# Expert products taken two at a time with biases laid by matmuls, routing weights broadcast through DRAM, and the router's marks kept in PSUM

## What is computed

```python
logits = xt @ Wr + br                                  # 64 -> 8
probs = softmax(logits); top_p, top_idx = top_k(probs, 2)
weights = top_p / top_p.sum(axis=-1, keepdims=True)
xe = layernorm(xt)[None] * ln_g[:, None] + ln_b[:, None]
h = gelu(einsum('end,edh->enh', xe, W1) + b1[:, None])  # 64 -> 256, all 8 experts
y = einsum('enh,ehd->end', h, W2) + b2[:, None]         # 256 -> 64
out = (weights[:, :, None] * y_of_the_two_experts).sum(axis=1)
```

## Time and profile before

| | us |
|---|---|
| median of 3 runs | 408.23 (407.21 to 408.71) |
| the profiled execution, its own time | 409.93 |
| its span in the profile | 408.2 |
| VectorE busy | 337.5 (83%) |
| TensorE busy | 338.1 (83%) |
| ScalarE busy | 281.3 (69%) |
| GpSimd busy | 265.9 (65%) |
| all DMA queues, share of 16 engines | 62.7% |

### The profile page before, as it was taken

One profiled execution on the slowest core, in us unless ns is written; L12 is line 12 of the kernel. 1 busy time (PEld: TensorE's weight loads), 2 busy tenths in 40 slices (PEclk: granted clock), 3 DMA queues, 4 the chain that ended last, 5 costly groups with the idle time before them and its releaser, 6 DMA issues. The chain is left out here.

```text
span 408.2 us, 5461 instructions
## 1 busy us (share of the span) xinstructions
PE 338.1 (83%) x1642; PEld 181.1 (44%) x1642; DVE 337.5 (83%) x462; ACT 281.3 (69%) x458; POOL 265.9 (65%) x270
## 2 busy tenths in 40 slices
PE   0597897677999789888988997899789878998694
PEld 0484445333454445344534552455245424544352
DVE  2774458998999999999999999999999988995411
ACT  1002667498978987998799879987887757761462
POOL 9706112986569947994898589758975984593122
PEclk9996999589899999999999999999988986999899
DMA  8761079899899588658975697579667950000000
GB/s 195 204 134 26 2 189 223 216 227 224 203 222 227 138 206 205 163 123 197 219 177 137 153 239 169 146 174 220 151 162 176 230 124 0 2 0 13 2 0 13
DMA packets 21236, 59.52 MB, mean 146 GB/s; under 512 B 4924, under 2 KB 13272, under 8 KB 15320
## 3 DMA queue, kind: packets, MB, share of 16 engines
q1 hardware_dynamic: 20040, 58.34, 61.7%
q10 hardware_dynamic: 1168, 0.84, 0.8%
HBM read 53.93 MB, written 5.24 MB: 145 GB/s over the span
## 5 line engine op out<-in xcount | busy, mean ns | idle before, releaser
L345 POOL TENSOR_TENSOR hs<-hs,Cs 128x1024 f32<-128x1024 f32 x63 | 149.2, 2372 | 44.9 <-DVE hs L767 44.3
L767 DVE TENSOR_TENSOR_SCAN hs<-av,P 128x1024 f32<-128x1024 f32 x64 | 146.3, 2287 | 4.7 <-ACT av L576 1.3
L633 ACT ACTIVATE hb<-P,b1c 128x512 f32<-128x512 f32 x128 | 81.6, 684 | 18.8 <-PE P L1177 16.3
L760 DVE SCALAR_TENSOR_TENSOR P<-P,bbcol,ub 128x1024 f32<-128x1024 f32 x62 | 79.7, 1286 | 2.4 <-DMA ub<-u_scratch 1.2
L1190 PE MATMUL P<-hb,W2s 128*64 128x256 f32 x512 | 70.0, 397 | 0.0
L1176 PE MATMUL P<-X,W1H 128*128 128x512 f32 x128 | 60.4, 472 | 6.4 <-ACT hb L633 4.7
L576 ACT ACTIVATE av<-P,Aneg 128x510 f32<-128x510 f32 x68 | 44.1, 688 | 13.9 <-PE P L1130 10.0
L1177 PE MATMUL P<-X,W1L 128*128 128x512 f32 x128 | 52.3, 409 | 0.0
L357 POOL TENSOR_TENSOR accs<-accs,mes 128x256 f32<-128x256 f32 x56 | 40.9, 731 | 14.1 <-DVE mes L856 9.5
L1190 PEld LDWEIGHTS P<-hb,W2s 128*64 128x64 f32 x512 | 31.8, 138 | 31.4 <-issue 20.8
L856 DVE SCALAR_TENSOR_TENSOR mes<-P,cols,wbs 128x256 f32<-128x256 f32 x64 | 27.3, 468 | 17.4 <-PE P L1190 9.6
(11 more groups left out here) (190 smaller groups left out, 488.8 us busy)
## 6 DMA issues: line engine op xcount, KB each, us to landing
ub<-u_scratch SPq DMA_DIRECT2D x31, 1024.0 KB, 10.7
av<-dt_scratch SPq DMA_DIRECT2D x15, 1024.0 KB, 7.0
dt_scratch<-dts SPq DMA_DIRECT2D x7, 256.0 KB, 2.8
u_scratch<-rl SPq DMA_DIRECT2D x7, 256.0 KB, 2.8
av<-in_L_conv_Wr SPq DMA_DIRECT2D x2, 576.0 KB, 7.3
av<-in_L_conv_Wl SPq DMA_DIRECT2D x2, 576.0 KB, 8.1
res<-in_x SPq DMA_DIRECT2D x4, 256.0 KB, 4.8
hb<-in_L_ffn_W SPq DMA_DIRECT2D x2, 512.0 KB, 6.3
```

The lines of the kernel that those rows point to most:

```text
L345: gp.tensor_tensor(hs[:, at, :, :], hs[:, at, :, :], rep(Cs[:, p, :], 1, 2), ALU.mult).then_inc(S["cm"], 1)
L633: a_.activation(hb[:, r % 4, :], P[:, (XA, XB)[r % 2], :], ACT.Gelu, bias=b1c[:, r:r + 1]).then_inc(S["gl"], 1)
L760: v.scalar_tensor_tensor(out=ring, in0=rep(P[:, BB, :], 1, 2), scalar=bbcol[:, 0:1], in1=ub[:, 2 * n:2 * n + 2, :], op0=ALU.add, op1=ALU.m ...
L767: v.tensor_tensor_scan(hs[:, (SLOTS * g + n) % RING].rearrange("p a t -> p (a t)"), av[:, 2 * n:2 * n + 2, :].rearrange("p a t -> p (a t)" ...
```

## The change

Five things are done.

1. **Expert products.** One product with 512 columns takes the place of two with 256. The bias is no longer added there: TensorE opens each bank with a matmul of `b2w` by `b2sel` (64 rows, f32r, 512 columns), and the four matmuls of each of the four half steps add to it. `b2w` holds each bias in a high and a low part; both are built in the setup, from four more small DMAs and some 15 more VectorE instructions.
2. **Broadcast of the weights.** `selW`, the eight matmuls and the four ScalarE copies per body go. TensorE transposes the plain weights, ScalarE copies them to `wT` (16 x 256) and issues a DMA to `w_scratch` in DRAM. SP waits for its landing and issues six DMAs that fill `wbs` from it (1 MB in all), between piece 0 and piece 1 of the scan's loads. VectorE waits for the first two (`wb0`) at the first pair of experts, the next two (`wb1`) at the second, the last two (`wb2`) at the third.
3. **Router's marks.** The exponential and the ranked marks are written to PSUM (`chances`, `ranked`, in bank XC).
4. **Router's bias.** A matmul of `ident` by `brs` opens the bank, and the two logit matmuls add to it; L816 goes.
5. **Order.** The router's maximum and difference stand between the two halves of `X`; the layer norm product of group i+2 (`xnt<-P,rs`) stands inside the router. GpSimd's split of the weights (two instructions) goes.

```diff
@@ SP: sp_spread, and a new function
             for c in range(CHUNKS):
+                if c == 1 and g >= 2:
+                    sp_weights(sp_, g - 2)
                 since(sp_, "scan", SLOTS * (g - 1) + 2 * c + 2)
...
+        def sp_weights(sp_, g):
+
+            sp_.wait_ge(S["wt_out"], 16 * (g + 1))
...
+            since(sp_, "me", PAIRS * g)
+            for r, (lo, hi) in enumerate(((0, 2), (2, 4), (4, 8))):
+                for h in range(2):
+                    sp_.dma_start(wbs[64 * h:64 * h + 64, lo:hi, :],
+                                  rep(w_dram[g % 2][EXP * h + lo:EXP * h + hi, :], 0, 64)).then_inc(S[f"wb{r}"], 16)
@@ GpSimd: pool_router
+            since(eng, "wtr", 2 * g)
             gp.tensor_tensor(rt[:, 11], rt[:, 10], rep(rv[:, 5], 2, EXP), ALU.mult).then_inc(S["wn"], 1)
-            eng.wait_ge(S["wn"], g + 1)
-            w4 = rt[:, 11].rearrange("p (q h) e -> p q h e", h=2)
-            since(eng, "wtr", 2 * g)
-            gp.tensor_copy(vv[:, :, :, 0, :].bitcast(f32r), w4).then_inc(S["vhi"], 1)
-            eng.wait_ge(S["vhi"], g + 1)
-            gp.tensor_tensor(vv[:, :, :, 1, :], w4, vv[:, :, :, 0, :], ALU.subtract).then_inc(S["vlo"], 1)
@@ ScalarE
-            a_.activation(rt[:, 2], rt[:, 1], ACT.Exp).then_inc(S["ex"], 1)
+            a_.activation(chances, rt[:, 1], ACT.Exp).then_inc(S["ex"], 1)
...
-            a_.activation(wT[:, :], P[0:32, XD, 0:HW], ACT.Copy).then_inc(S["wtc"], 1)
-
-        def act_wb(eng, g, r):
-            eng.wait_ge(S["wb_mm"], EXP * g + 2 * r + 2)
-            if r == 0:
-                since(eng, "me", EXP * g)
-            a_.activation(wbs[:, 2 * r:2 * r + 2, :].rearrange("p e f -> p (e f)"), P[:, YS, :], ACT.Copy).then_inc(S["wb"], 1)
+            since(eng, "wt_out", 16 * g)
+            a_.activation(wT[:, :], P[0:2 * EXP, YS, 0:HW], ACT.Copy).then_inc(S["wtc"], 1)
+            eng.wait_ge(S["wtc"], g + 1)
+            since(eng, "wb2", 32 * (g - 1))
+            eng.dma_start(w_dram[g % 2], wT[:, :]).then_inc(S["wt_out"], 16)
@@ VectorE
+                if h == 1 and between is None:
+                    dve_router1(eng, g)
                 v.tensor_tensor(X2[0:64, HW * h:HW * h + HW], P[q, XB, 0:HW], rqs[q, :], ALU.mult).then_inc(S["xh2"], 1)
...
-            v.tensor_tensor(biased, P[:, XC, 0:4 * EXP].rearrange("p (c e) -> p c e", e=EXP),
-                            rep(brs[:, :], 1, 4), ALU.add).then_inc(S["lgb"], 1)
...
-            v.scalar_tensor_tensor(out=rt[:, 3], in0=rt[:, 2], scalar=1.0, in1=rank[:, :, :], op0=ALU.is_ge, op1=ALU.mult).then_inc(S["s1"], 1)
+            v.scalar_tensor_tensor(out=ranked, in0=chances, scalar=1.0, in1=rank[:, :, :], op0=ALU.is_ge, op1=ALU.mult).then_inc(S["s1"], 1)
...
             v.tensor_reduce(rv[:, 2], rt[:, 5], AX, ALU.max).then_inc(S["m2"], 1)
+            if norm is not None:
+                dve_xn(eng, norm)
...
-            v.scalar_tensor_tensor(out=mes[:, e % 4, :], in0=P[:, (XC, XD)[e // 2 % 2], HW * (e % 2):HW * (e % 2) + HW],
-                                   scalar=cols[:, R["b2"] + e:R["b2"] + e + 1], in1=wbs[:, e, :],
-                                   op0=ALU.add, op1=ALU.mult).then_inc(S["me"], 1)
+            j = e // 2
+            eng.wait_ge(S["f2"], EXP * KC * g + 2 * KC * (j + 1))
+            eng.wait_ge(S[f"wb{min(j, 2)}"], 32 * (g + 1))
+            since(eng, "acc", EXP * g + max(e - 2, 0))
+            v.tensor_tensor(mes[:, 2 * (j % 2):2 * (j % 2) + 2, :].rearrange("p e f -> p (e f)"), P[:, (XC, XD)[j % 2], :],
+                            wbs[:, e:e + 2, :].rearrange("p e f -> p (e f)"), ALU.mult).then_inc(S["me"], 1)
@@ TensorE
             eng.wait_ge(S["cs"], so_far(g, 3))
+            pe.matmul(P[:, XC, 0:4 * EXP], ident[:, :], rep(brs[:, :], 1, 4), start=True, stop=False).then_inc(S["lgb"], 1)
...
-            for e in (2 * r, 2 * r + 1):
-                pe.matmul(P[:, YS, HW * (e % 2):HW * (e % 2) + HW], selW[:, e, :], wT[:, :],
-                          start=True, stop=True).then_inc(S["wb_mm"], 1)
...
+                pe.matmul(P[:, (XC, XD)[pair % 2], :], b2w[:, pair, :], b2sel, start=True, stop=False).then_inc(S["bias"], 1)
```

More of the change, by code:

```diff
@@ L204, in build @@
         rT, at = within(buf1, at, [B, NODES])
-        selWf, at = within(buf1[0:32], at, [EXP, 2, 64])
+        b2all, at = within(buf1, at, [128])
+        b2hi, at = within(buf1, at, [128])
+        b2st, b2hi = b2all[64:128], b2hi[64:128].bitcast(f32r)
+        b2w = b2t[64:128, 0:4, :]
+        b2sel = b2t[64:128, 4:8, :].rearrange("p e f -> p (e f)")
         Wfs, at = within(buf1, at, [HW])
@@ L304, in _ @@
                     sp_.dma_start(rows[R[name]:R[name] + n, 64 * h:64 * h + 64], ap).then_inc(S["ld_rows"], 16)
-            sp_.wait_ge(S["k_zero"], 8)
+            sp_.wait_ge(S["k_b2"], 1)
+            for k in range(2):
+                for h in range(2):
+                    sp_.dma_start(b2st[32 * k:32 * k + EXP, 64 * h:64 * h + 64], b2).then_inc(S["ld_b2"], 16)
+            sp_.wait_ge(S["k_zero"], 7)
             for h in range(2):
@@ L739, in _ @@
                     act_wt(eng, G - 1)
-                if n in range(2, 6):
-                    act_wb(eng, G - 1, n - 2)
         ring = P[:, 0:2, :]
@@ L1005, in body @@
                     dve_xn2(eng, prev)
-                    dve_router1(eng, prev)
-                    dve_router2(eng, prev)
-                if i > 0 and nxt2 is not None:
-                    dve_xn(eng, nxt2)
+                    dve_router2(eng, prev, nxt2)
                 dve_slot(eng, i, 2)
@@ L1041, in _ @@
             dve_router2(eng, G - 1)
-            for e in range(EXP):
+            for e in range(0, EXP, 2):
                 dve_expert(eng, G - 1, e)
@@ L1182, in pe_f2 @@
             pair = r // (2 * KC)
[L1183 to L1188 removed]
+            if r % (2 * KC) == 0:
+                if r == 0:
+                    eng.wait_ge(S["e2"], g + 1)
+                if r == 2 * KC:
+                    eng.wait_ge(S["xn1"], so_far(g, 4))
+                if pair >= 2:
+                    eng.wait_ge(S["me"], PAIRS * g + pair - 1)
+                pe.matmul(P[:, (XC, XD)[pair % 2], :], b2w[:, pair, :], b2sel, start=True, stop=False).then_inc(S["bias"], 1)
             for h in range(2):
                 last = pe.matmul(P[64 * h:64 * h + 64, (XC, XD)[pair % 2], HW * (e % 2):HW * (e % 2) + HW], W2s[:, e, k, :],
[L1191 removed]
+                                 hb[:, r % 4, HW * h:HW * h + HW], start=False, stop=(k == KC - 1 and e % 2 == 1))
             last.then_inc(S["f2"], 1)
@@ L1367, in body @@
                     pe_f2(eng, prev, 1)
-                    for n in range(2, 6):
-                        pe_pair(eng, prev, n)
-                        pe_wb(eng, prev, n - 2)
-                    for n in range(6, 8):
+                    for n in range(2, 8):
                         pe_pair(eng, prev, n)
@@ L1407, in _ @@
             pe_f2(eng, G - 1, 1)
-            for n in range(2, 6):
-                pe_pair(eng, G - 1, n)
-                pe_wb(eng, G - 1, n - 2)
-            for n in range(6, 9):
+            for n in range(2, 9):
                 pe_pair(eng, G - 1, n)
```

112 lines of the change are left out of this document (54 added, 58 removed).

## The result

The changed kernel takes 414.54 us (median of 5 runs, 412.41 to 416.67); the kernel before took 408.71 beside it (5 runs, 407.21 to 410.58). The ratio is 1.0136, 95% interval 1.0091 to 1.0181: slower by 5.5 us, little but clear of noise, where 4.6 us faster was forecast and everything over 410 us was given a chance of 0.13. The profiled execution of after is the fastest of its five (412.41, span 410.7), so its trace shows only 2.5 us of the loss. Times and ratios here leave out slow executions, more than 1.5% above the fastest of their kernel: one of f1_pe_nobias, and two of e3b_first, its profiled one among them. The time splits at the gate products G (line L798 now) as follows; the last two lines are later experiments.

The account below looks back on a forecast made before the run. VectorE was taken to set the body, with GpSimd's chain nearly equal from slot 5 to the gate. Terms -1.4 - 4.9 - 1.1 + 2.8 = -4.6 us gave 403.6 us, range 399.3 to 408.8.

Parts of the forecast that it names:

- Marks in PSUM: VectorE's ranked marks (L829) in the router would take 0.19 us instead of 895 ns on average, 4.9 us over seven bodies.
- Pair products and GpSimd's chain: Expert products: 0.15 us saved per pair, only the first pair counting in six bodies because GpSimd's chain binds; 1.4 us.
- Router's bias and order: Router in each body: removing L816 and reordering only lengthen the wait for the exponential; zero, -0.1 to +0.2 a body.
- The broadcast in a steady body: DRAM trip of the weights: wb0 there at G + 20.7, wanted at G + 21.6; 0.9 us of slack, no wait.
- rival A: Weights' round trip late in every body; 1.1 us late in six bodies adds 6.6, 410.2 us. A or B in full 0.13.
- Body 1: The queue is behind there, so the first expert product waits 2.8 us for wb0, once; bounds 0 and 4.
- What TensorE sheds, and the biases: Eight matmuls, four ScalarE copies and two GpSimd instructions go per body: zero in bodies; tail bias matmuls 0.23 us each, +0.9.
- Tail and setup: Tail 1.1 us shorter, from spread steps -1.7 and bias matmuls +0.9 among others; setup zero, at most 0.6.
- B: Rival: DMA queue becomes the bound with 64-partition loads at half rate; 407, or 410 with body 1's wait; in full, with A, 0.13.
- D: Rival: the marks stay slow, the 4.9 us gain goes, 408.5 us; with partial A or B, 0.21.
- C: Rival: body 1 does not stall (400.8 us), or GpSimd's chain yields as well (398.0); chance 0.14.

Follow-up runs that it names:

- f1_pe_nobias: The kernel of e2b_pe without the four bias matmuls per body, the biases b2 left out of the computation: 403.41 us, ratio 0.9874 to the kernel before.
- e3b_first: The changed kernel with, in body 1 only, the six weight loads issued ahead of piece 0: 414.23 and 419.95 us, ratio 1.0241 to the kernel before.
- f3_router: The kernel before with marks in PSUM, router's bias by matmul and the new order; no pairs, expert biases or DRAM: 401.3 us, ratio 0.9852.
- f4_thin: The changed kernel with each load of wbs filling only 16 of its 64 partitions: 408.51 us, ratio 0.9987 to the kernel before.
- f2_after_nobias: The changed kernel, DRAM trip kept, without the bias matmuls, b2 left out of the computation: 414.45 us, ratio 1.0151 to the kernel before.
- e2b_pe: The changed kernel with weights spread by TensorE and copied by ScalarE again, nothing through DRAM: 413.77 us, ratio 1.0159 to the kernel before.

## Why the prediction was wrong, point by point

**Marks in PSUM: right.** They take 0.20 us in all bodies and shorten a mean body by 0.78 us when alone (forecast 0.70).

**Pair products and GpSimd's chain: right.** f1_pe_nobias is f3_router with pairs and without the additions of `b2`. Its mean body is 38.71 - 38.55 = 0.16 us shorter; 0.15 was forecast, since only the first pair lies ahead of GpSimd's chain. The gates of after wait 0.7 us and more, as forecast, and f4_thin shows GpSimd behind that. Whether the pairs pay as a whole can't be told: the ratios of f1_pe_nobias and f3_router, 0.9874 and 0.9852, lie well within each other's intervals. In the profiled executions f1_pe_nobias is longer in body 1 (39.8 against 39.0 us), from G7 to G8 (38.0 against 36.8) and from there to the end (36.1 against 34.5), each time beside a lower granted clock (the share of full speed): 0.91 against 0.95 and 0.90 against 0.99 in the last two. In body 1 it is low right behind the gate. The same stretch in f1_pe_nobias and in f3_router (columns as in the earlier trace rows):

```profile
95.12:101.70 6.58, 5.67 (x17) 3.52 (x18) 5.32 (x7) 4.85 (x11) 5.76 (x4) 0.74 1.01 229
...
95.48:102.00 6.52, 5.18 (x20) 2.79 (x20) 6.17 (x8) 6.31 (x14) 5.64 (x4) 1.00 1.01 225
```

There VectorE waits 0.94 us for the layer norm, which runs over TensorE; in f3_router it does not. That speaks for the clock and not the pairs as the cause; what lowers the clock in one execution and not in another, no run took apart.

**Router's bias and order: a little too cautious.** Zero was forecast, with -0.1 at best; -0.2 a body came.

**"The broadcast in a steady body": the step that failed.** It put `wb0` at G + 20.7, 0.9 us before it is wanted. In body 3 (G at 178.79) the write is issued at G + 15.1, as forecast. It lands at G + 18.7: 3.55 us instead of 2.5, over the upper bound of 3.2. The loads are there 201.34 - 197.45 = 3.9 later, instead of 0.55 + 2.4 = 2.95. Together G + 22.55, and VectorE wanted it at 201.34 - 1.11, G + 21.4. The lateness is 1.1 us, the very case of rival A, which gave 410.2. It came in bodies 3 and 4, and with 1.8 us in body 6; in bodies 2 and 5 no such wait shows. Both bounds came from rows of DMAs that had the queue to themselves; the same 64 KB store that took 2.1 us takes 3.8 in the fuller queue of after. The number for it had been in the text: piece 0, issued at 222.32, lands 10.7 later, at G + 18.8 (the prediction rounds to 18.9). It was used as an argument for the rival and not as a term, although it is the landing time of the write to within 0.2 us. The 2 us of HBM access at high load that the rival drew from the Trainium skill ("DMA: Bandwidth & Descriptors", section "Latency and other measured facts") leaned the right way, but it isn't the mechanism: the time depends on what is ahead.

Not all that bodies 2 to 6 lost is this wait. They are 5 x (39.94 - 38.8) = 5.7 us longer than forecast, and 4.0 of these are waits for `wbs`. The rest goes with VectorE's waits for the layer norm behind the gate, 0.4 us in body 2 and 0.9 in body 4, and 0.8 for TensorE in body 5. In body 4 the granted clock was low there, and the write was issued 1 us later than in body 3. VectorE's wait, then the stretch behind the gates of body 4 and body 3:

```profile
225.24 0.42 DVE L808 TENSOR_TENSOR tns<-P,rs2s 128x256 f32<-128x256 f32 x1 [0.92 <-ACT rs2s L608]
```

```profile
218.85:225.24 6.39, 5.65 (x18) 3.81 (x19) 5.32 (x5) 4.01 (x9) 6.04 (x5) 0.73 0.49 123
...
178.79:185.10 6.31, 5.18 (x20) 2.80 (x20) 6.15 (x8) 5.91 (x13) 6.00 (x5) 1.00 0.87 208
```

**Body 1: right place, half the size.** 2.8 us were forecast, 5.88 came. The prediction put the load of `wbs` behind piece 0 and let it land 1.2 us after it. But SP may issue that load only when the write has landed, and the write itself stands behind piece 0. So one landing (117.9) is followed by a whole DMA (3.7), and the product, wanted at 115.7, starts at 121.6. The bound of "4 if the write to DRAM is late too" took the lateness of the write for a side case. Behind the late product VectorE waits once more for TensorE, 0.35 and 0.69 us in the last slots.

**What TensorE sheds, and the biases.** "Zero in the bodies" is right for the kernel as changed (f2_after_nobias, f4_thin). But a bias matmul takes 0.42 us, not 0.23: it was priced like an f32r matmul that follows another of its kind, as in the earlier trace rows, where the first of such a series also took longer (390.03 to 390.38, 0.35). The 1.7 us a body fit into TensorE's list only because four spread steps of 0.42 left it; with both, e2b_pe is as slow as the changed kernel. In the tail the biases cost 1.7 instead of 0.9. Of the four versions, only the one without either is fast (us, ratio to before):

| | with bias matmuls | without |
|---|---|---|
| weights through DRAM | 414.54, 1.0136 (after) | 414.45, 1.0151 (f2_after_nobias) |
| weights by TensorE | 413.77, 1.0159 (e2b_pe) | 403.41, 0.9874 (f1_pe_nobias) |

**Tail and setup.** From G8 to the end it is 36.2 - 34.3 = 1.9 us shorter (1.1 forecast), and from G7 to G8 38.9 - 37.1 = 1.8, where the forecast had 0.70 for the marks and 0.45 for three pairs. Both are mild misses on the good side, but f4_thin, with the same instructions there, took 35.6 and 38.0, so these stretches scatter by more than the misses. The half steps of the tail repeat in 2.1 and 2.6 us, the longer one with the bias in it. The setup gave 0.7 us (up to 0.6 was forecast), which can't be told from none: the first G lies at 93.3 to 95.4 in three kernels with the same setup (after, f2_after_nobias, f4_thin).

**The rivals.** A's steady part came true in three of the bodies 2 to 6, with body 1 on top of it. B did not: the DMA share is 0.79 to 0.86 in the bodies 2 to 5, where full rate made it 34.8 / 38.9 = 0.89, and the writes wait for one piece, not for a queue that falls behind. Share times length went from 30 us a body before to 33 in these: the added megabyte took some 3 us, not the 9.2 of half rate. The 248 GB/s of the earlier trace rows, the argument against B, are not of the `res` loads alone, since ScalarE's queue issued weight loads in the same microseconds. D fell with the marks, C with body 1.

**The sum.** Piece by piece, forecast against the two profiled executions (us, minus is shorter):

| | to first G | body 1 | bodies 2 to 6 | G7 to G8 | tail | sum |
|---|---|---|---|---|---|---|
| forecast | 0 | +1.9 | -4.2 | -1.2 | -1.1 | -4.6 |
| measured | -0.7 | +5.7 | +1.3 | -1.7 | -2.0 | +2.5 |

So body 1 and bodies 2 to 6 together missed by 9 us, and 2 came back elsewhere. The medians lie 5.8 us apart and not 2.5, because after was profiled in its fastest execution, 2.1 below its median, and before 1.2 above the median it was compared with. Where the slower executions of after lose this, no trace shows. The parts do not add up either: marks (-3.9), router (-2.2), the DRAM trip alone (+9.0) and pairs with biases (+12, f3_router to e2b_pe) make +15, where +5.5 to +6 was measured. The table of four versions shows one reason: beside the spread steps the biases cost 10 us, but the DRAM trip takes these steps off TensorE, and beside it the biases cost nothing in the bodies. And once the wait for the DMA sets the body, what other parts save is mostly spent in it.

## What to carry to other kernels

A round trip through DRAM that crosses a busy queue is to be priced from the queue, not from its size: here its first leg landed behind the loads that another engine had issued earlier, and only then did the second leg start. Before an engine's work is called free, count what it must also take on in the same change: here four matmuls of 0.42 us fitted only into the place of the four steps that went. Changes with several parts should be timed part by part, and in pairs where two could hide each other: three of the five parts here (marks, router's bias, order) gave 6 to 7 us, one took 9 alone, and undoing that one alone gave nothing back, since the biases then bound.

## What the runs showed of the hardware

- A 16 KB write by ScalarE's queue landed 1.4 to 2.1 us after its issue with nothing ahead, 2.3 in body 1 with piece 0 issued behind it, 8.2 with the 2 MB of piece 0 issued 3 us earlier.
- The marks with one input and the output in PSUM: 200 ns in 8 of 8 cases, 7 of them beside a busy GpSimd, where the form with both inputs in SBUF had a mean of 895.
- A bias matmul of 512 columns between matmuls of another kind held TensorE 0.42 us, where one behind its own kind held it 0.23.
- Loads to 64 partitions did not run at half rate: see rival B above. The half rate of the Trainium skill's "SBUF — State Buffer", section "Door 1: The DMA port swizzle", doesn't show in this case, in which the loads fill the two halves in turn; none was run on one half alone.
